# Dealing the late layout of a mixture's blocks out between the chunks of its first blocks

## The chip, the cores and the metric

One core of one Trainium2 chip. The metric is the device time of one launch in microseconds (us), the median of the runs shown. In the profile the engines are PE (TensorE, matmuls), PEld (its weight loads), DVE (VectorE), ACT (ScalarE), POOL (GpSimd) and SP (SyncE, which here mostly issues DMAs).

## The reference

x is 4 x 1024 x 128, float32. A layer normalisation feeds a mixture of experts, an attention follows, and then the same mixture again:

```python
x = x + 0.5 * ffn(layernorm(x))
x = x + attn(layernorm(x))
x = x + 0.5 * ffn(layernorm(x))
```

`ffn` normalises its rows once more, computes eight router logits a token, keeps the two largest, and adds the two experts' outputs weighted by a softmax of the two. An expert (D = 128, H = 512) normalises, then computes

```python
x1 = x @ W1 + b1
x2 = clip(x @ W2 + b2, -20, 20)
hidden = clip(x1 * (x2 * sigmoid(x2)), -10000, 10000)
return clip(hidden @ Wo + bo, -10000, 10000)
```

`attn` is an attention of 16 heads of 8 in which queries, keys and values are the same projection.

## The kernel before, in words

**Routing.** The first mixture routes its 4096 tokens in four batches of 1024 (`first_routing`, four jobs of 13 steps). For each token and choice DVE works out the place of its row, and POOL scatters 128 rows at a time to DRAM (L1296, 16 scatters a batch), where each expert has a region of its own. All engines run the same list of steps in the same order, each doing its own part.

**Blocks.** The rows are then worked off in 40 blocks: blocks 0 to 22 and 31 to 39 of 256 rows, blocks 23 to 30 of 128. Which expert and which rows a block takes depends on the routing. DVE works it out on one partition and leaves it in `whose_i`, where SP reads it into a register for the two loads of a block, the expert's weights (`ffn_rec`, L958, four slots in this mixture) and the rows (`ffn_block_rows`, L963, six slots).

**The two layouts.** `vector_lay_out_early` lays out blocks 0 to 16 (`EARLY` = 17) from the counts of the first three batches. `vector_lay_out_late` lays out blocks 17 to 39 from the counts of all four. It has nine pieces (`share(part, 9)`), 47 small DVE instructions, most of them on one partition and 8 to 46 elements, a few on up to 368. Most wait for the one before it: `settle` adds a semaphore signal to an instruction and makes DVE wait for it. Piece 0 begins with `end_i` (L1790), which signals `laid_out`; SP waits for that before the fillers of blocks 8 to 15. Piece 8 ends with `whose_i` (L1871), which signals `laid_out` again; SP waits for that before the loads of block 17. Its buffers are small tiles of their own and one partition of two routing buffers that nothing else uses in that time.

In the program before, DVE runs the whole late layout in one go, behind the last routing step and ahead of `vector_experts(0)`.

**A block.** `tensor_experts`, `scalar_experts` and `vector_experts` go through the 40 blocks, with four chunks of the hidden units in each (c = 0 to 3). The order on each engine is fixed:

- PE, block i: chunk 0 (two products, L2188 and L2190), turn back block i-2 (L2210), turn block i+1 (L2141), chunks 1 and 2, second product of block i-1 (L2200, eight matmul records), chunk 3. A chunk has one of four PSUM banks and waits until the combination of four chunks before has emptied it.
- DVE, block i: clip of chunk 0 (L1917), combination of block i-1's chunk 3 (L1928), clip of block i-1's hidden units (L1936), clip of chunk 1, combination 0, clip 2, combinations 1 and 2, clip of block i-1's y (L1943), clip 3.
- ACT: the silu of each chunk (L1455), the copy of the turned rows (L1409), the bias (L1464) and the weighting (L1473) of y.
- POOL: scatters the finished rows of y (L1312), two blocks behind.

The second product of block i-1 waits for the clipped hidden units, these for the combination of chunk 3, that for the silu of chunk 3, and that for the clip of chunk 3.

**Chores.** Between the chunks each engine calls `tail(k, i, c)`: a list of chores for mixture k, block i, ahead of chunk c. For the first mixture the lists are `HEAD`, for blocks 1 to 39, with index 4 * (block - 1) + c. Before the change they hold the last batch's 14 remaining scatters, the wait for the first turned blocks, the blanking of attention's buffers from block 16 on, and, from block 31, the beginning of attention. A chore is a tuple (what, which, step, part); each engine does what it has for it, and the chore "lay" is known to DVE alone (`vector_chore`), with which = 0 for the early and 1 for the late layout. In the second mixture the lists are `TAIL`, with index 4 * block + c, and the late layout is already dealt out there, one piece in each of the slots 40, 42, ... 56, that is, ahead of chunks 0 and 2 of blocks 10 to 14.

Of the kernel before, what the change touches and what calls it, by code (L numbers as in the profile page):

```python
# [88 lines left out]
def build_macaron(nc, x, w_qkv, w_o, ln_g, ln_b, router_w, eg, eb, w1, b1, w2, b2, wo, bo, out):  # L89
# [83 lines left out]
    with stack:  # L173
# [509 lines left out]
        HEAD = [[] for _ in range(HC * (BLOCKS - BEGIN))]  # L683

        def plan_head(block, slots):
            for slot, what, which, step in slots:
                HEAD[HC * (block - BEGIN) + slot].append((what, which, step, WHOLE))
# [3 lines left out]
        FIRST_OUT = 2  # L691
        for block in range(BEGIN, BEGIN + 3):
            plan_head(block, [(0, "turned", block, 0)])
        for n in range(FIRST_OUT, BT * TOPK):
            HEAD[HC * (n - FIRST_OUT)].append(("route", JOBS[B - 1], ROUTE_STEPS - 1, (n, BT * TOPK)))
        plan_head(16, [(HC * n, "blank", n, 0) for n in range(6)])
# [70 lines left out]
        def first_routing():  # L767

            def steps(b, which):
                if b < B:
                    for k in which:
                        yield "route", JOBS[b], k, WHOLE

            def scatters(b, part):
                yield "route", JOBS[b], SCATTER, (part, 6)

            def folds(pieces):
                for n in pieces:  # L780
                    if n <= E:
                        yield "fold", n, 0, WHOLE

            yield from steps(0, range(6))
            yield from steps(1, (0,))
            yield from steps(0, (6,))
            yield from steps(1, (1,))
            yield from steps(0, range(7, SCATTER))
            yield from folds((0,))
            for b in range(1, B):  # L790
                yield from steps(b, (2,))
                yield from folds((3 * b - 2,))
                yield from scatters(b - 1, 0)
                yield from steps(b, (3, 4))
                yield from scatters(b - 1, 1)
                yield from steps(b, (5,))
                yield from folds((3 * b - 1, 3 * b))
                yield from steps(b + 1, (0,))
                yield from steps(b, (6,))
                yield from scatters(b - 1, 2)  # L800
                yield from steps(b + 1, (1,))
                yield from steps(b, (7,))
                yield from scatters(b - 1, 3)
                yield from steps(b, (8, 9))
                if b == B - 1:
                    yield "folded", 0, 0, WHOLE
                yield from scatters(b - 1, 4)
                yield from steps(b, (10, 11))
                if b == B - 2:
                    yield "lay", 0, 0, WHOLE  # L810
                yield from scatters(b - 1, 5)
# [753 lines left out]
        def settle(instruction):  # L1565
            instruction.then_inc(dve_own.sem, 1)
            V.wait_ge(dve_own.sem, dve_own.up())

        def vector_program():
            V.wait_ge(pool_made, 3)  # L1570
            V.tensor_copy(region[:, :], regions[:, :])
            V.tensor_copy(block_f[:, :], blocks_i[:, 0, :])
            V.tensor_copy(tile_f[:, :], blocks_i[:, 1, :])
            settle(V.tensor_reduce(out=order[:, :], in_=not_later[:, :, :].rearrange("p i j -> p j i"), axis=AX.X, op=ALU.add))
            settle(V.memset(running[:, :, :], 1.0))
            V.memset(running[:, :, 0:1], 0.0)
            V.memset(twice[:, :], 1.0)
            V.memset(skipped[:, :, :], 0.0)
            V.memset(ends[:, :, 0:1], 0.0).then_inc(dve_made, 1)
            V.wait_ge(dve_made, 1)  # L1580
            for what, which, step, part in first_routing():
                if what == "route":
                    vector_route(which, step, part)
                elif what == "lay":
                    vector_lay_out_early()
                elif what == "folded":
                    vector_fold()
            vector_lay_out_late()
            vector_experts(0)
            vector_attention()  # L1590
            vector_experts(1)
            vector_last_sums()

        def vector_fold():
            V.wait_ge(fold_act, 1)
            V.wait_ge(fold_pe, 1 + E)
            bias = [record[:, :, at:at + HC] for at in (BIAS1, BIAS2)]
            for k in range(2):
                V.tensor_tensor(bias[k], wide[1][:, k * 512:k * 512 + E * HC].rearrange("p (e c) -> p e c", c=HC),
                                b_col[k].rearrange("p (e c) -> p e c", c=HC), ALU.add).then_inc(fold_dve, 1)  # L1600
            V.wait_ge(fold_dve, 2)
            V.tensor_copy(record[:, :, BO], bo_col)
            V.tensor_scalar(record[:, :, CLIP_LO:CLIP_LO + HC], bias[1], -1.0, -X2_LIMIT,
                            ALU.mult, ALU.add).then_inc(fold_dve, 1)
            V.tensor_scalar(record[:, :, CLIP_HI:CLIP_HI + HC], bias[1], -1.0, X2_LIMIT,
                            ALU.mult, ALU.add).then_inc(fold_dve, 1)
# [150 lines left out]
        def vector_lay_out_early(part=WHOLE):  # L1757


            for at in share(part, 8):  # L1760
                if at == 0:
                    settle(V.tensor_tensor(tiles_f[:, :], carry[0:1, :], region[0:1, :], ALU.subtract))
                    V.tensor_copy(tiles_i[:, :], tiles_f[:, :])
                    settle(V.tensor_scalar(firsts_f[:, :], first_rows[:, :], float(BLOCK - 1), None, ALU.add))
                    settle(V.tensor_copy(firsts_i[:, :], firsts_f[:, :]))
                elif at == 1:
                    V.tensor_scalar(firsts_i[:, :], firsts_i[:, :], BLOCK.bit_length() - 1, None,
                                    ALU.logical_shift_right)
                    settle(V.tensor_scalar(pairs_i[:, :], tiles_i[:, :], BLOCK.bit_length() - 1, None,
                                           ALU.logical_shift_right))  # L1770
                    V.tensor_copy(pairs_f[:, :], pairs_i[:, :])
                    settle(V.tensor_copy(firsts_f[:, :], firsts_i[:, :]))
                elif at == 2:
                    vector_pairs(0, EARLY)
                elif at == 3:
                    V.tensor_tensor(taken[:, :], got[:, 0:E], got[:, E:2 * E], ALU.add)
                    settle(V.tensor_tensor(skipped[:, 0, E:2 * E], ends[:, 0, E:2 * E], got[:, 0:E], ALU.subtract))
                    settle(V.tensor_copy(skipped[:, 0, 0:E], ends[:, 0, 0:E]))
                    settle(V.tensor_scalar(skipped[:, 0, :], skipped[:, 0, :], float(BH), None, ALU.mult))
                elif at < 7:  # L1780
                    vector_places_of_blocks(at - 3, 0, 1)
                else:
                    vector_whole_places(0, 1)
# [94 lines left out]
        def vector_experts(k):  # L1878
            if k == 0:

                V.wait_ge(fold_act, 1 + E)
                V.wait_ge(fold_dve, 4)
                for job in JOBS[1:B - 1]:
                    for lane in set_of(job).rows_out:
                        V.wait_ge(lane, 16 * BT)
            for i in range(BLOCKS):
                vector_tail(k, i, 0)
                vector_clip(k, i, 0)
                if i:
                    vector_combine(k, i - 1, 3)  # L1890
                    vector_clip_hidden(k, i - 1)
                vector_tail(k, i, 1)
                vector_clip(k, i, 1)
                vector_combine(k, i, 0)
                vector_tail(k, i, 2)
                vector_clip(k, i, 2)
                vector_combine(k, i, 1)
                vector_combine(k, i, 2)
                if i:
                    vector_clip_y(k, i - 1)  # L1900
                vector_tail(k, i, 3)
                vector_clip(k, i, 3)
            vector_combine(k, BLOCKS - 1, 3)
            vector_clip_hidden(k, BLOCKS - 1)
            vector_clip_y(k, BLOCKS - 1)
# [488 lines left out]
```

## Time and profile before

| | |
|---|---|
| median of 3 runs | 1370.96 us (1369.79, 1370.96, 1371.23) |
| the profiled execution | 1381.39 us |
| its span (first to last instruction) | 1379.3 us |
| mean granted TensorE clock | 0.978 |
| PE busy | 1245.2 us (90%) |
| DVE busy | 1156.8 us (84%) |
| ACT busy | 893.9 us (65%) |
| POOL busy | 534.9 us (39%) |
| chain that ended last, by engine | PE 57%, DVE 21%, issue 10%, ACT 4%, DMA 3%, SP's queue 3% |

The profiled execution is one run of its own and 10 us longer than the median of the others. Its times are counted from the first instruction. In it the first mixture's blocks begin at about 105 us, attention at about 340 us, and the second mixture's late layout is worked off between 1195 and 1224 us. A row of the trace has the start of an instruction or a group of them, its duration, its engine and its line, what it writes and reads, and, in brackets, how long the engine sat idle ahead of it and what ended that. Instructions of one engine overlap a little in these rows.

### The profile page before, as it was taken

The page shows a single profiled execution, that of the slowest core. Times are in us where ns is not written, and L with a number is a line of the kernel's source. Part 1 is how long each engine was busy: PE and PEld are TensorE (multiplying, and loading weights), DVE is VectorE, ACT ScalarE, POOL GpSimd, SP SyncE. Part 2 cuts the span into 40 slices and gives each one's busy share as a digit, 9 for nine tenths or more (in the row PEclk, how much of TensorE's full clock was granted, in tenths as well). Part 3 has the DMA queues.
Part 4 walks back from the last instruction along what each step waited for, and adds up shares of the span by engine and source line. Part 5 has one row for each costly group of instructions (what it writes and reads, how often), then busy time and mean ns, then how long its engine had stood idle before and what let it go on. Part 6 is the DMA issues. An engine that isn't in the chain of part 4 may idle for free.

```text
span 1379.3 us, 29625 instructions
## 1 busy us (share of the span) xinstructions
PE 1245.2 (90%) x10053; PEld 645.8 (47%) x10053; DVE 1156.8 (84%) x2354; ACT 893.9 (65%) x1881; POOL 534.9 (39%) x665
## 2 busy tenths in 40 slices
PE   3738999888699999999999999999999989999993
PEld 3737888776123223322323323233322247778882
DVE  8768888787998998889898888988899647988885
ACT  1214555554288888888788787788877874555651
POOL 3872557253542002234234424333443215553332
PEclk9999999999599999999999999999999999999996
DMA  8125655553212200112011011011100222555653
GB/s 272 42 70 186 208 206 189 214 190 104 72 37 60 67 28 12 36 38 73 19 45 49 13 59 37 21 33 54 36 3 20 104 82 105 189 186 200 232 209 131
DMA packets 65383, 135.58 MB, mean 98 GB/s; under 512 B 13330, under 2 KB 34932, under 8 KB 65204
## 3 DMA queue, kind: packets, MB, share of 16 engines
q1 hardware_dynamic: 56052, 115.39, 24.5%
q0 software_dynamic: 8704, 16.93, 3.7%
q8 instruction: 83, 1.36, 0.4%
q10 hardware_dynamic: 480, 1.38, 0.3%
q14 instruction: 64, 0.52, 0.1%
HBM read 47.35 MB, written 25.07 MB: 53 GB/s over the span
## 4 chain that ended last, share of the span: by engine, by line
PE 57%; DVE 21%; issue 10%; ACT 4%; DMA 3%; SPq 3%; POOL 1%; DVEq 0%; ACTq 0%; another core or an unknown queue 0%; POOLq 0%
PE psum L2290 14%; DVE att_neg_part L1976 11%; PE psum L2266 8%; PE psum L2200 7%; PE psum L2188 6%; PE psum L2190 6%; PE psum L2270 5%; PE psum L2247 5%; DMA ffn_block_rows<-rows_dram 2%; DVE att_neg_part L1981 2%; DVE ffn_x2c L1917 2%; DVE ffn_hidden L1928 1%; DVE stats L1610 1%; ACT att_probs L1488 1%; PE psum L2313 1%
## 5 line engine op out<-in xcount | busy, mean ns | idle before, releaser
L1488 ACT ACTIVATE att_probs<-psum 128x512 f32<-128x512 f32 x1024 | 556.3, 596 | 118.5 <-PE psum L2272 88.4
L1976 DVE TENSOR_REDUCE att_neg_part<-psum 128x2 f32<-128x1024 f32 x443 | 534.9, 1223 | 59.3 <-PE psum L2248 45.9
L2290 PE MATMUL psum<-att_probs,att_values 128*16 128x256 f32 x4096 | 320.3, 385 | 6.2 <-ACT att_o_t L1503 4.0
L1455 ACT ACTIVATE ffn_silu<-ffn_x2c,ffn_rec 128x256 f32<-128x256 f32 (+1 forms) x320 | 154.9, 487 | 173.0 <-DVE ffn_x2c L1917 128.1
L1312 POOL DMA_INDIRECT y_dram<-ffn_y,ffn_block_rows x144 | 143.7, 998 | 239.8 <-ACT ffn_y L1473 203.6
L2247 PE MATMUL psum<-att_right,att_left 64*128 64x512 bf16 x512 | 197.9, 388 | 13.6 <-DVE att_neg_part L1976 8.5
L2269 PE MATMUL psum<-att_right,att_left 64*128 64x512 bf16 x512 | 198.9, 388 | 4.2 <-DVE att_neg_part L1976 2.5
L2266 PE MATMUL psum<-att_right,att_left 64*128 64x512 bf16 x512 | 198.9, 388 | 4.1 <-DVE att_neg_part L1976 3.7
L2248 PE MATMUL psum<-att_right,att_left 64*128 64x512 bf16 x512 | 198.4, 388 | 0.0
L2270 PE MATMUL psum<-att_right,att_left 64*128 64x512 bf16 x512 | 193.9, 379 | 0.0
L2272 PE MATMUL psum<-att_right,att_left 64*128 64x512 bf16 x512 | 193.7, 378 | 0.0
L1917 DVE TENSOR_SCALAR ffn_x2c<-psum,ffn_rec 128x256 f32<-128x256 f32 (+1 forms) x320 | 162.8, 513 | 36.7 <-PE psum L2190 29.4
L2188 PE MATMUL psum<-ffn_block_t,ffn_rec 128*128 128x256 f32 (+1 forms) x640 | 179.6, 363 | 1.3 <-ACT ffn_block_t L1409 1.3
L1296 POOL DMA_INDIRECT rows_dram<-rows,place_i x128 | 126.6, 989 | 135.6 <-PE psum L2272 85.7
L2190 PE MATMUL psum<-ffn_block_t,ffn_rec 128*128 128x256 f32 (+1 forms) x640 | 178.9, 361 | 0.0
L2290 PEld LDWEIGHTS psum<-att_probs,att_values 128*16 128x16 f32 x4096 | 68.1, 94 | 221.9 <-issue 151.6
L1928 DVE SCALAR_TENSOR_TENSOR ffn_hidden<-psum,ffn_rec,ffn_silu 128x256 f32<-128x256 f32 (+1 forms) x320 | 144.3, 451 | 19.0 <-ACT ffn_silu L1455 11.9
L2200 PE MATMUL psum<-ffn_hidden,ffn_rec 128*128 128x256 f32 (+1 forms) x640 | 142.7, 367 | 14.3 <-DVE ffn_hidden L1936 10.6
L2266 PEld LDWEIGHTS psum<-att_right,att_left 64*128 64x128 bf16 x512 | 47.4, 93 | 196.7 <-ACT att_probs L1488 124.6
L1214 POOL TENSOR_TENSOR att_max_rest<-att_max_rest,att_max_parts 16x128 f32<-16x128 f32 x64 | 26.7, 417 | 276.8 <-ACT att_max_parts L1562 274.0
L2200 PEld LDWEIGHTS psum<-ffn_hidden,ffn_rec 128*128 128x128 f32 x640 | 112.0, 193 | 36.0 <-DVE ffn_hidden L1936 18.6
L2190 PEld LDWEIGHTS psum<-ffn_block_t,ffn_rec 128*128 128x128 f32 x640 | 118.2, 193 | 13.5
(222 smaller groups left out, 1522.3 us busy)
## 6 DMA issues: line engine op xcount, KB each, us to landing
ffn_rec<-record SPq DMA_DIRECT2D x80, 776.5 KB
ffn_block_rows<-rows_dram SPq DMA_DIRECT2D x64, 130.0 KB
att_left<-q_parts_dram SPq DMA_DIRECT2D x64, 96.0 KB
att_right<-q_parts_dram SPq DMA_DIRECT2D x124, 48.0 KB
record<-in_L_ffn_W SPq DMA_DIRECT2D x16, 256.0 KB, 6.4
att_right<-q_parts_dram SPq DMA_DIRECT2D x92, 32.0 KB
y_dram<-ffn_y,ffn_block_rows POOLq DMA_INDIRECT x144
q_parts_dram<-att_parts SPq DMA_DIRECT2D x12, 192.0 KB
```

The costliest lines, as they stand in the source:

```text
L1488: S.activation(probs[:, slot % PROBS, :], ring_bank(("score", slot))[:, :], ACT.Exp, scale=SCALE).then_inc(att_bank.by_act, 1)
L1976: last = V.tensor_reduce(out=neg_part[:, h % 2, keys, p::PAIR, t], in_=psum[:, low:high + 1, :], axis=AX.X, op=ALU.max, negate=True)
L2188: TE.matmul(both[:, few], mix[k].rec[:, s, W2 + c * P:W2 + (c + 1) * P], mix[k].block_t[:, m % 2, few], start=True, stop=True)
L2190: TE.matmul(both[:, w1_few], mix[k].rec[:, s, W1 + c * P:W1 + (c + 1) * P], mix[k].block_t[:, m % 2, few], start=True, stop=True).then_inc ...
L2200: last = TE.matmul(y_bank[n % 2][:, few], mix[k].rec[:, s, WO + c * F:WO + (c + 1) * F], mix[k].hidden[:, n % 2, c, few], start=(c == 0), ...
L2247: TE.matmul(bank[low], left[s][TOP, p, q], right[s][TOP, p, k], start=True, stop=True)
L2248: TE.matmul(bank[high], left[s][BOTTOM, PAIR + p, q], right[s][BOTTOM, PAIR + p, k], start=True, stop=True).then_inc(maxed, 1)
L2266: TE.matmul(low, left[s][TOP, p, k], right[s][TOP, p, q], start=True, stop=False)
L2269: TE.matmul(high, left[s][BOTTOM, PAIR + p, k], right[s][BOTTOM, PAIR + p, q], start=True, stop=False)
L2270: TE.matmul(low, left[s][TOP, PAIR + p, k], right[s][TOP, PAIR + p, q], start=False, stop=True).then_inc(att_bank.filled, 1)
L2272: TE.matmul(high, left[s][BOTTOM, p, k], right[s][BOTTOM, p, q], start=False, stop=True).then_inc(att_bank.filled, 1)
L2290: last = TE.matmul(value_bank[head * VS:head * VS + VW, q], values[:, b % 2, kt, team * TEAM + head, :], probs[:, (UNIT * n + j) % PROBS, ...
```

## The change

The call of `vector_lay_out_late` ahead of the blocks goes. In its place nine chores ("lay", 1, 0, (k, 9)) are appended to the lists 1, 6, 11, 16, 21, 26, 31, 36 and 41 of `HEAD`.

```diff
         FIRST_OUT = 2
         for block in range(BEGIN, BEGIN + 3):
             plan_head(block, [(0, "turned", block, 0)])
+        for k in range(9):
+            HEAD[1 + 5 * k].append(("lay", 1, 0, (k, 9)))
         for n in range(FIRST_OUT, BT * TOPK):
             HEAD[HC * (n - FIRST_OUT)].append(("route", JOBS[B - 1], ROUTE_STEPS - 1, (n, BT * TOPK)))
...
                     vector_lay_out_early()
                 elif what == "folded":
                     vector_fold()
-            vector_lay_out_late()
             vector_experts(0)
             vector_attention()
             vector_experts(1)
```

## Rows read from the trace of the kernel before

**Rows 1.** Stretch, us; busy PE, PEld, DVE, ACT, POOL; granted clock, DMA share, GB/s.

```profile
135.00:152.00 17.00, 17.00 (x87) 14.98 (x86) 14.07 (x32) 9.94 (x25) 8.80 (x9) 1.00 0.58 204
```

**Rows 2.** Timeline of DVE, 95 to 114 us: start, duration, instruction.

```profile
96.16 0.37 DVE L1790 CAST end_i<-carry 1x8 int32<-1x8 f32 x1
...
105.73 0.15 DVE L1813 TENSOR_TENSOR skipped<-ends,taken 1x8 f32<-1x8 f32 x1
...
106.96 0.22 DVE L1849 TENSOR_TENSOR xf_t<-block_f,ends 1x96 f32<-1x96 f32 x1
...
108.22 0.52 DVE L1855 TENSOR_REDUCE whose<-xf_t 1x23 f32<-1x368 f32 x1
...
109.34 0.17 DVE L1859 TENSOR_SCALAR of_the_second_half<-whose 1x23 f32<-1x23 f32 x1
...
110.64 0.17 DVE L1867 TENSOR_SCALAR whose<-whose 1x23 f32<-1x23 f32 x1
...
111.52 1.04 DVE L1917 TENSOR_SCALAR ffn_x2c<-psum,ffn_rec 128x256 f32<-128x256 f32 x2
...
113.61 0.55 DVE L1917 TENSOR_SCALAR ffn_x2c<-psum,ffn_rec 128x256 f32<-128x256 f32 x1 [0.49 <-PE psum L2190]
```

**Rows 3.** Timeline of PE, 109 to 118 us.

```profile
109.58 0.69 PE L2141 MATMUL psum<-identity,ffn_block_rows 128*128 128x128 f32 x2 [0.91 <-DMA ffn_block_rows<-rows_dram]
...
117.51 1.99 PE L2200 MATMUL psum<-ffn_hidden,ffn_rec 128*128 128x256 f32 x8 [0.27 <-DVE ffn_hidden L1936]
```

**Rows 4.** The chain that ended last, in order of time: start, us, what.

```profile
115.13 0.55 DVE ffn_x2c L1917
...
116.24 0.50 DVE ffn_hidden L1928
116.76 0.70 DVE ffn_hidden L1936
...
129.02 1.73 PE psum L2200 x8
```

**Rows 5.** Timeline of DVE in a block without a chore, 126 to 132 us.

```profile
126.03 0.54 DVE L1917 TENSOR_SCALAR ffn_x2c<-psum,ffn_rec 128x256 f32<-128x256 f32 x1
126.89 0.54 DVE L1917 TENSOR_SCALAR ffn_x2c<-psum,ffn_rec 128x256 f32<-128x256 f32 x1 [0.32 <-PE psum L2190]
127.35 0.47 DVE L1928 SCALAR_TENSOR_TENSOR ffn_hidden<-psum,ffn_rec,ffn_silu 128x256 f32<-128x256 f32 x1
127.86 0.69 DVE L1936 TENSOR_SCALAR ffn_hidden<-ffn_hidden 128x1024 f32<-128x1024 f32 x1
...
131.29 0.29 DVE L1943 TENSOR_SCALAR ffn_y_t<-ffn_y_t 128x256 f32<-128x256 f32 x1 [0.38 <-ACT ffn_y_t L1464]
131.65 0.54 DVE L1917 TENSOR_SCALAR ffn_x2c<-psum,ffn_rec 128x256 f32<-128x256 f32 x1
```

**Rows 6.** Timeline of DVE in the second mixture, pieces 0, 1 and 2.

```profile
1195.81 0.15 DVE L1790 CAST end_i<-carry 1x8 int32<-1x8 f32 x1
...
1196.88 0.54 DVE L1917 TENSOR_SCALAR ffn_x2c<-psum,ffn_rec 128x256 f32<-128x256 f32 x1
...
1199.31 0.14 DVE L1798 SCALAR_TENSOR_TENSOR tiles_f<-taken,tiles_f 1x8 f32<-1x8 f32 x1
...
1200.82 0.54 DVE L1917 TENSOR_SCALAR ffn_x2c<-psum,ffn_rec 128x256 f32<-128x256 f32 x1
...
1203.00 0.14 DVE L1835 TENSOR_TENSOR pairs_in_order<-firsts_f,pairs_f 1x8 f32<-1x8 f32 x1
...
1203.97 0.54 DVE L1917 TENSOR_SCALAR ffn_x2c<-psum,ffn_rec 128x256 f32<-128x256 f32 x1
```

**Rows 7.** Timeline of PE in the second mixture, two second products.

```profile
1198.60 1.99 PE L2200 MATMUL psum<-ffn_hidden,ffn_rec 128*128 128x256 f32 x8 [1.26 <-DVE ffn_hidden L1936]
...
1205.69 1.99 PE L2200 MATMUL psum<-ffn_hidden,ffn_rec 128*128 128x256 f32 x8 [0.63 <-DVE ffn_hidden L1936]
```

**Rows 8.** POOL's row scatters, 88 to 103 us: ns min/median/max, first and last start.

```profile
L1296 POOL DMA_INDIRECT rows_dram<-rows,place_i x12: 954/958/961, 88.0 to 101.9; - x12
```

## The prediction

> **What bounds the kernel now.** I read the stretch around the change first, then the place the change writes to, then a later stage of the same program that already does what the change asks for. In blocks 3 to 6 of the first mixture PE is busy 17.00 of 17 us and DVE 14.07 [rows 1]: PE is the bound, a block takes it 5.62 us (from one clip of chunk 3 to the next, 131.65 - 126.03 [rows 5]), and DVE has under a fifth of each block to spare. Ahead of the blocks DVE is alone with the late layout, from 96.16 on; its first clip starts at 111.52, right behind it [rows 2]. So the layout looks as if it held the mixture up. It doesn't: PE has nothing to multiply until block 0's rows land, it then waits 0.91 us for block 1's rows, by DMA [rows 3], and DVE, once in the loop, waits 0.49 us for PE at the clip of chunk 2 (113.61 [rows 2]). From there the order of the work is the same with or without the layout.
>
> **What the change removes.** 15.36 us of DVE in one piece (96.16 to 111.52 [rows 2]). What it uncovers: chunk 0's product ended at 108.67 (109.58 - 0.91 [rows 3]), so the first clip may start 2.85 us earlier. The next ones, and the first silu and combination, move up too, but the clip of chunk 2 needs a product that came later than DVE did, by 0.49 us. Everything behind (the silu, the chunk 3 clip at 115.13, the combination at 116.24 [rows 4], the clipped hidden block, PE's second product at 117.51 [rows 3]) hangs on that clip. I cost the gain at 0. Its bounds are 0 and 2.85 us. The SP queue's loads of the first four blocks wait for the early layout and for scatters, not for this one; the fillers and block 17 do wait for it, and it ends in block 11, so five blocks (28 us) ahead of the last of those needs. The layout's two signals to SP move with it; no DMA and no PE, ACT or POOL instruction does.
>
> **What it adds.** The same instructions, in nine pieces, in front of a clip each. Block and chunk by the index 1 + 5k: piece 0 in block 1 chunk 1, then 2/2, 3/3, 5/0, 6/1, 7/2, 8/3, 10/0, 11/1. Their lengths, from first instruction to the next clip: the second mixture deals out the same nine pieces, and there pieces 0, 1, 2 take 1.07 (1196.88 - 1195.81), 1.51 (1200.82 - 1199.31) and 0.97 us (1203.97 - 1203.00) [rows 6]. The others from the layout itself [rows 2]: pieces 3 and 4 together 1.23 (106.96 - 105.73), piece 5 1.26, piece 6 1.12, piece 7 1.30, piece 8 0.88. For pieces 0 to 2 the layout's own rows give 9.57 us (105.73 - 96.16) instead of 3.55: that stretch has pauses between tiny instructions that the second mixture has not. I take the dealt-out lengths, because the work around them is the same; the other value is the upper end.
>
> **What covers a piece.** In a block without one [rows 5]: 0.32 us of waiting for PE before the clip of chunk 0, 0.38 us before the clip of y, 0.07 us between that and the clip of chunk 3. A row that reads PSUM reaches 0.08 into the next when they are packed (126.89 + 0.54 against 127.35), so these are room for 0.40, 0.46 and 0.15. Between the clip of chunk 3 and its combination lie 1.32 us (127.35 - 126.03), where the fastest is 1.11 (116.24 - 115.13 [rows 4]): a late clip of chunk 3 recovers only 0.21 on that way. Last, the hidden block is clipped at 128.55 (127.86 + 0.69 [rows 5]) and PE wants it at 129.02 [rows 4]; 0.05 goes to the signal (116.76 + 0.70 [rows 4] is followed by 117.51 [rows 3]), so 0.41 or 0.42 is slack; I take 0.41. The room is therefore
> - ahead of chunk 1 or 2: 0.46 + 0.15 + 0.21 + 0.41 = 1.23;
> - ahead of chunk 3: 0.15 + 0.21 + 0.41 = 0.77;
> - ahead of chunk 0: 0.40 + 0.41 = 0.81.
>
> What is over stops PE; after a stop DVE is still 0.41 late, which the next block takes back if nothing comes first. Queued behind a piece on DVE are exactly this clip, the silu of ACT and, last, PE's second product.
>
> **A test of this rule.** In the second mixture piece 1 stands ahead of a chunk 2 and piece 2 ahead of the following chunk 0, DVE coming in 0.41 late. The rule says 0.41 + 1.51 - 0.46 - 0.15 = 1.31, then - 0.40 + 0.97 = 1.88, then - 0.41 = 1.47 us of stop. PE's second products start at 1198.60 and 1205.69 [rows 7]: 7.09 - 5.62 = 1.47.
>
> **The sum.** Piece 0: DVE comes in late by 0.15 (its slack of 0.41 is used up by the stop of 0.27 before 117.51, and PE's slow restart, 1.99 against 1.73 for the eight products [rows 3, 4], gives 0.26 back). 0.15 + 1.07 = 1.22, under 1.23: no cost, 0.40 stays open. Piece 1: 0.40 + 1.51 - 1.23 = 0.68. Piece 2: the open 0.41 is taken back ahead of the clip of y, 0.97 - 0.77 = 0.20. Pieces 3 and 4: at most 0.7 each, covered by 0.81 and 1.23. Piece 5: 1.26 - 1.23 = 0.03. Piece 6: 1.12 - 0.77 = 0.35. Piece 7: 1.30 - 0.81 = 0.49. Piece 8: 0.88, covered. Together 1.75. A restart of PE costs 0 to 0.26 (1.99 - 1.73); the row of a packed group overlaps its neighbours, so I take 0.10, and count it for pieces 2, 6 and 7, where no further piece follows at once: 0.30. **Sum +2.05 us**, against the profiled execution's 1381.39 us (span 1379.3). The median of the runs is 1370.96, 10.4 us lower; the stage is PE-bound in both, so I carry the term over unchanged: 1370.96 + 2.05 = 1373.0. Nothing later has room to take it back: every later stage starts from the blocks before it. A measurement of this kernel can tell about 0.2%, 2.7 us, from no change, so the forecast lies just inside "no change".
>
> **A rule weighed.** Of POOL's twelve row scatters between 88 and 103 us the first seven run ahead of the layout and the others beside it, and all take the same: 954 to 961 ns [rows 8]. The layout doesn't hold them up, so nothing is released when it goes. The Trainium skill (SBUF — State Buffer, "Who interferes with whom") says that a DVE copy, cast or tensor_scalar in a mode that uses two ports locks GpSimd out for the whole instruction, which would delay its writing of descriptors. By that rule the start would gain; the trace does not bear it out here.
>
> **Rivals.**
> 1. *Slower: the pauses come along.* Pieces 0 to 2 keep the length they have in the layout, 9.57 us for 3.55, and the 6.02 us more go straight to PE, since the room is used up: +2.05 + 6.02 = 8.1, 1379.0. For it: the pauses sit in exactly these instructions. Against: the same instructions have none in the second mixture, nor pieces 3 to 8 in the layout. It decides as soon as a piece in blocks 1 to 3 is 0.7 us longer than taken. Chance 0.14.
> 2. *Faster: the early first clip counts.* If PE's pace or its second product follows DVE after all, the 2.85 us come through: 1370.2 with the pieces' cost, 1368.1 if those are hidden too. Against: the 0.49 us wait at 113.61 and PE's wait for DMA at 109.58. Chance 0.08.
> 3. *All pieces hidden.* DVE's share of 14.07 in 17 leaves 0.97 us a block, 10.7 us in eleven blocks, more than the 9.3 us of pieces. By the average they fit: 1371.0. Against: the test above, where spare time that lies behind the hidden block doesn't help it. Chance 0.09.
> 4. *The scatters were held.* The five scatters beside the layout, freed of up to 0.37 us each (its first instruction [rows 2]), would bring the rows 1.9 us earlier: 1373.0 - 1.9 = 1371.1. Against: rows 8. The Trainium skill's rule above is this case. Chance 0.03.
>
> **How the numbers follow.** The forecast has 0.66. Its own spread is the restart (0 to 0.26 five times) and some 0.1 a piece, from +1.3 to +3.5, so about a quarter of it lies above +2.7. Slower by over 0.2%: 0.14 + 0.66 x 0.24 = 0.30. Faster by over 0.2% (under 1368.2): half of rival 2, 0.04. Within: 0.66. The range goes from 1369.8 (rivals 3 and 4, less the 1.2 us by which a run of before lies under the median) to 1376.5 (the forecast's upper end and half of what rival 1 adds).
>
> **What would show it.** DVE's first clip near 108.7 us and PE's first second product still at 117.5; no PE wait in blocks 1, 4, 6 and 11; waits of PE for the hidden block of 0.5 to 0.8 us by piece 1 (block 2's second product), and of 0.2 to 0.6 us behind pieces 2, 6 and 7; attention starting 2 us later. It is wrong if PE's second product of block 0 moves, if PE has no stop by piece 1, or if a piece in blocks 1 to 3 lasts over 2 us.

## The result, and the profile after

The changed kernel takes **1374.20 us**, the median of eight runs (1372.89 to 1377.16), and the kernel before 1370.27 us, the median of eight beside them (1368.70 to 1373.86). The ratio is 1.003, with a 95% interval from 1.0018 to 1.0042, so the change costs 3.9 us, between 2.5 and 5.8. That is slower by more than 0.2%, the case that had 0.30. The time lies inside the range, 1.2 us above the forecast; the forecast's sum of 2.05 us is about half of what was lost. That the time itself came so close is in part luck: beside it the kernel before took 0.7 us less than the 1370.96 us that the forecast started from.

The profiled execution of the changed kernel took 1375.75 us, span 1373.7. This is **less** than the 1381.39 us (span 1379.3) of the profiled execution of before, while the medians stand the other way round. So the two profiles can't be subtracted as wholes; they have to be compared stage by stage. The top of the page of the changed kernel:

```profile
span 1373.7 us, 29625 instructions
PE 1245.5 (91%) x10053; PEld 644.2 (47%) x10053; DVE 1154.9 (84%) x2354; ACT 893.3 (65%) x1881; POOL 533.2 (39%) x665
```

The instruction counts are those of before and the busy times differ by 2 us at most. The change shows only in where the engines stand idle. The windows view of the eleven blocks and a little behind them (stretch; busy PE, PEld, DVE, ACT, POOL; granted clock, DMA share, GB/s) has PE idle for 2.36 us of 77 where the same stretch of the kernel before, in a second profile of it taken later (run e10_before), has 0.26. After:

```profile
113.00:190.00 77.00, 74.64 (x365) 63.34 (x364) 68.78 (x175) 42.06 (x105) 35.40 (x36) 1.00 0.56 191
```

Before, second profile:

```profile
113.00:190.00 77.00, 76.74 (x381) 67.45 (x381) 63.65 (x138) 44.42 (x108) 37.25 (x38) 1.00 0.57 196
```

The view of waits names what stopped PE in that stretch of the changed kernel (us in total, times, longest):

```profile
PE psum L2201 <- DVE ffn_hidden L1937: 1.6, 3, 0.6
PE psum L2211 <- DVE ffn_y_t L1944: 0.8, 1, 0.8
```

Three of the four are waits of the second product for the clipped hidden block, as the prediction had them. The fourth, the longest, isn't: PE's turn back waits for the clipped y. Both are on PE's timeline (start, duration, instruction, idle before it and its releaser). Each second product is the eight matmuls of one block:

```profile
112.40 1.99 PE L2201 MATMUL psum<-ffn_hidden,ffn_rec 128*128 128x256 f32 x8 [0.26 <-DVE ffn_hidden L1937]
118.13 1.91 PE L2201 MATMUL psum<-ffn_hidden,ffn_rec 128*128 128x256 f32 x8
...
122.53 0.44 PE L2211 MATMUL psum<-identity,ffn_y_t 128*128 128x128 f32 x2 [0.77 <-DVE ffn_y_t L1944]
124.77 1.99 PE L2201 MATMUL psum<-ffn_hidden,ffn_rec 128*128 128x256 f32 x8
...
131.16 2.00 PE L2201 MATMUL psum<-ffn_hidden,ffn_rec 128*128 128x256 f32 x8 [0.51 <-DVE ffn_hidden L1937]
...
160.68 1.99 PE L2201 MATMUL psum<-ffn_hidden,ffn_rec 128*128 128x256 f32 x8 [0.49 <-DVE ffn_hidden L1937]
...
167.16 1.99 PE L2201 MATMUL psum<-ffn_hidden,ffn_rec 128*128 128x256 f32 x8 [0.60 <-DVE ffn_hidden L1937]
```

These groups make a clock for the stage. An undisturbed block lasts 5.62 us from the end of one group to the end of the next ([rows 5] give the same period from DVE). Block 2's ends at 126.76 and block 1's at 120.04: 6.72 us, an **excess** of 1.10. Summed over blocks 1 to 11 the excess is 4.2 us. In both profiles of the kernel before it is zero there. A second profile of the changed kernel, taken later (e11_after), gives 4.25 us, block for block within 0.08. Nothing takes it back up to block 24: from block 0's group to block 24's it is 130.79 and 130.77 us in the two profiles of before, 134.99 and 135.03 in the two of the changed kernel. From block 25 on, two profiles of one and the same kernel differ by 0.7 to 3.9 us in this measure, so they can't follow it further. The runs lost 3.9 us, which agrees with it.

The start of the blocks is the other place to look. In the profile of before, PE's first turn began at 105.40 and the first second product at 117.51 [rows 3], 12.11 us later. Here PE reads

```profile
102.65 0.66 PE L2142 MATMUL psum<-identity,ffn_block_rows 128*128 128x128 f32 x2 [12.26 <-DMA ffn_block_rows<-rows_dram]
```

and the second product is at 112.40, 9.75 us later; PE turns block 1 at 105.78 without the 0.91 us wait for its rows. One of the prediction's signs of being wrong has come up: "if PE's second product of block 0 moves". Read alone, this says that the change won 2.4 us at the start and lost 6.3 us in the blocks.

### The profile page after: what moved, and what is told of

Same layout as the page of the kernel before. It is cut to its first block, busy times and chain, and to the rows that moved or that the text cites. A ratio compares the mean times of both kernels' runs of the same rounds, so it can differ in the third digit from the quotient of the medians.

```text
span 1373.7 us, 29625 instructions
## 1 busy us (share of the span) xinstructions
PE 1245.5 (91%) x10053; PEld 644.2 (47%) x10053; DVE 1154.9 (84%) x2354; ACT 893.3 (65%) x1881; POOL 533.2 (39%) x665
## 4 chain that ended last, share of the span: by engine, by line
PE 56%; DVE 25%; issue 5%; POOL 5%; ACT 4%; DMA 4%; SPq 1%; DVEq 0%; ACTq 0%; POOLq 0%
PE psum L2291 14%; DVE att_neg_part L1977 11%; PE psum L2267 8%; PE psum L2201 7%; PE psum L2189 5%; PE psum L2191 5%; PE psum L2271 5%; PE psum L2248 5%; POOL rows_dram L1298 3%; DVE ffn_x2c L1918 2%; DMA ffn_block_rows<-rows_dram 2%; DVE att_neg_part L1982 2%; DVE ffn_hidden L1929 2%; DVE stats L1611 1%; ACT ffn_silu L1457 1%
```

## The experiments

Two readings had to be told apart, and one more came up on the way.

- **Theory A**, the prediction's: the layout ahead of the blocks costs nothing, and the whole loss is PE stopped by the dealt-out pieces. The quicker start in the profile is chance.
- **Theory B**: the layout in front does hold up the start, by 2.4 us (12.11 against 9.75), and the pieces cost 6.3. B2 is its small form, a gain of about 0.7 us.
- **Theory L**, formed on the changed kernel's trace: a scatter on POOL holds up DVE's clip of y, which reads and writes SBUF alone, if the clip comes at a bad moment, and pieces bring it there.

The level of the kernel before was different from one group of runs to the next (1370.3, 1379.6, 1388.5 and 1370.9 us). The last three groups ran on three different chips. Every time is therefore set against the runs of before of its own group. A kernel without any late layout (e1_none) was to measure the front part by itself; it gave no time and decides nothing.

### The pieces alone: e2_twice

The layout is called ahead of the blocks, as before, and the nine pieces are dealt out as well, as a repetition without signals.

```
+    vector_lay_out_late()                              # ahead of vector_experts(0)
-    HEAD[1 + 5 * k].append(("lay", 1, 0, (k, 9)))
+    HEAD[1 + 5 * k].append(("lay", 2, 0, (k, 9)))      # 2: vector_lay_out_late(part, signal=False)
```

> The late layout stands ahead of the blocks as before and is dealt out a second time in the changed kernel's places, the second time without its signals. This adds the pieces alone. Theory A: the same time as the changed kernel, +4.2 us to before, 1374.5, with the PE stops of the changed kernel (0.77 for the turn back, 0.5, 0.5 and 0.6 for the hidden block). Theory B: 2.4 us slower than the changed kernel, 1376.6.

Measured: 1382.46 us against 1379.58; ratio 1.0034, interval 1.0021 to 1.0047. Its excess is 4.22 us in the pattern of the changed kernel, and its start is that of before (12.24 us). The waits of PE in the blocks:

```profile
PE psum L2209 <- DVE ffn_hidden L1945: 1.8, 4, 0.6
PE psum L2219 <- DVE ffn_y_t L1952: 0.8, 1, 0.8
```

With the front part in place and the pieces added, the loss is the whole loss of the change. The ratio 1.0034 beside 1.003 leaves little room for a gain of 2.4 us from taking the front away.

### The pieces elsewhere, and finer: e3_chunk1, e4_fine

e3_chunk1 deals the same nine pieces ahead of chunk 1 of blocks 1 to 9, where the prediction's table has the largest room, 1.23 us:

```
-    HEAD[1 + 5 * k].append(("lay", 1, 0, (k, 9)))
+    HEAD[1 + 4 * k].append(("lay", 1, 0, (k, 9)))
```

> The same nine pieces, each ahead of chunk 1 of blocks 1 to 9. The prediction's rooms (1.23 us ahead of chunk 1) with the lengths of the changed kernel's trace (1.07, 1.69, 0.97, 0.61, 0.54, 1.38, 1.10, 1.28, 0.67) give 0.4 of lateness open from piece 0, then 0.86 for piece 1, 0.15 for piece 5, little for 7: about +1.2 us to before, with restarts of 0.26 each +1.8. If the pieces cost by their length and not by their place, it is +4.2 us as in the changed kernel.

Measured: 1380.60 us against 1379.58, ratio 1.0015 (1.0007 to 1.0024), excess 1.91 us. The waits:

```profile
PE psum L2211 <- DVE ffn_y_t L1944: 0.3, 1, 0.3
PE psum L2201 <- DVE ffn_hidden L1937: 0.3, 1, 0.3
```

Same work, same number of pieces, half the loss, by place alone. Piece 2 tells something more. It follows a stop, comes in 0.15 us late and lasts 0.98, together 1.13 us, under the room of 1.23, and still it costs 0.17.

e4_fine also goes to chunk 1, but in thirteen pieces: pieces 1, 5, 6 and 7 are each cut in two, so that none lasts longer than about 1.0 us.

```
+    for k in range(13):
+        HEAD[1 + 4 * k].append(("lay", 2, 0, (k, 13)))     # pieces 1, 5, 6 and 7 cut in two
```

> The layout in 13 pieces (pieces 1, 5, 6 and 7 cut in two), each ahead of chunk 1 of blocks 1 to 13, none longer than about 1.07 us. All are under the room of 1.23 us; with 0.28 us more for a DVE instruction that POOL holds up, only piece 0 may touch it. Theory A: the time of before, 1370.3 to 1371, and no PE stop over 0.2 us. Theory B: 2.4 us faster than before, 1367.9. If a piece costs whatever its length, +3 us or more.

Measured: 1377.14 us against 1379.58, ratio 0.9992 (0.9981 to 1.0004), excess 0.05 us in all, and one wait of PE in the stretch, the one ahead of block 0's second product that every kernel here has:

```profile
PE psum L2252 <- DVE ffn_hidden L1988: 0.2, 1, 0.2
```

The layout dealt out finely enough costs nothing, and brings nothing that this run can tell. Eleven more runs beside seventeen of the kernel before (e9_fine_again) narrow that down.

> The 13 short pieces once more, against the kernel before. Its nine stops are gone (0.05 to 0.2 us in the first look), so this measures what taking the layout from ahead of the blocks gives by itself. In the looks so far the way from the first turned rows to the first second product takes 12.1 to 12.2 us with the whole layout ahead and 9.8 to 11.7 without, and PE waits 0.8 to 1.0 us for block 1's rows with it and 0 to 0.4 without. Theory A (no gain; the differences are those of single executions): 0 to before, interval around it. Theory B2 (a small gain of some 0.7 us, which the changed kernel also has): -0.7 us. A gain of 2.4 us: -2.4 us.

Measured: 1370.64 us against 1370.89, ratio 0.9997 (0.9988 to 1.0006), excess 0.11 us. Under Theory B this kernel, with the front part gone and pieces that cost nothing, should have shown a gain of 2.4 us (0.9982); that lies outside the interval. B2's 0.7 us (0.9995) can't be excluded.

### The front doubled: e5_front_twice

The layout stands ahead of the blocks twice, and nothing is dealt out.

```
+    vector_lay_out_late()
+    vector_lay_out_again(WHOLE)        # the same, without signals; then vector_experts(0)
```

> The late layout runs twice in a row ahead of the blocks, the second time without its signals, nothing dealt out. It tells how much cover the place ahead of the blocks has. The second run's 47 instructions take 9.3 us where they aren't paused (the sum of the nine dealt-out lengths). If the cover is the 0.5 us by which DVE was early at the clip of chunk 2, DVE is late there by about 9 us and so is the first second product: about 21 us after the first turned rows, against 12.1 to 12.2 with one layout ahead; total +9 us. If DVE's work ahead of the blocks is hidden more deeply (behind PE's half pace or the loads), less than +5 us.

Measured in one run: 1392.59 us against a median of 1388.47 (1384.75 to 1392.52). The first second product comes 20.9 us after the first turn, 8.8 later than the 12.1 of before. PE's timeline:

```profile
108.04 0.66 PE L2149 MATMUL psum<-identity,ffn_block_rows 128*128 128x128 f32 x2 [12.39 <-DMA ffn_block_rows<-rows_dram]
...
124.52 1.19 PE L2196 MATMUL psum<-ffn_block_t,ffn_rec 128*128 128x256 f32 x2 [6.77 <-DVE ffn_hidden L1936]
...
128.51 0.59 PE L2198 MATMUL psum<-ffn_block_t,ffn_rec 128*128 128x256 f32 x2
128.94 1.89 PE L2208 MATMUL psum<-ffn_hidden,ffn_rec 128*128 128x256 f32 x8
```

So DVE in front does hold PE up once it is long enough: PE fills the banks that it has and stops at the next chunk. One layout ends before that point, two don't. After the stop of 6.77 us PE runs at half pace, two products in 1.19 us and then in 0.59. The windows of the two stretches show it in the granted clock, 0.50 (1.2 GHz) and 1.00 (2.4 GHz):

```profile
124.50:127.50 3.00, 2.98 (x8) 2.44 (x9) 2.55 (x6) 1.36 (x4) 0.00 (x0) 0.50 0.00 0
128.00:131.00 3.00, 3.00 (x16) 2.64 (x15) 2.55 (x6) 1.15 (x3) 0.00 (x0) 1.00 0.00 0
```

The one time is only 4.1 us above the median of its group, whose runs spread over 7.8 us; it decides nothing.

### Three pieces put back: e6_front3

Pieces 0 to 2 return to the front, the others stay dealt out.

```
+    for k in range(3): vector_lay_out_late((k, 9))     # ahead of vector_experts(0)
+    for k in range(3, 9): HEAD[1 + 5 * k].append(("lay", 1, 0, (k, 9)))
```

> Pieces 0 to 2 ahead of the blocks, pieces 3 to 8 dealt out where the change has them. By the stops in the changed kernel's trace pieces 3 to 8 make 2.1 of the 4.2 us (0.34 behind piece 5, 0.89 behind 6, 0.86 behind 7), so: +2.1 us to before, and no stop in blocks 1 to 5. By the prediction's terms: +0.9 and 0.2 of restarts, +1.1 us.

Measured: 1389.26 us against 1388.47, ratio 1.001 (0.9994 to 1.0026), excess 2.23 us: the stops of pieces 1 and 2 are gone, and those of 5, 6 and 7 stand unchanged (0.34, 0.90, 0.86). Another 0.12 is seen at block 4's second product, which stands behind chunk 0 of block 5, where piece 3 is (0.67 us long here). The pieces don't act on one another across the blocks without a piece between them.

### What stretches the clip of y: e7_act_out

The DVE timeline of the changed kernel has something that the one of before [rows 5] lacks. This is piece 1 and what follows it:

```profile
118.75 0.14 DVE L1799 SCALAR_TENSOR_TENSOR tiles_f<-taken,tiles_f 1x8 f32<-1x8 f32 x1
...
119.39 0.42 DVE L1805 CAST firsts_i<-firsts_f 1x8 int32<-1x8 f32 x1
...
120.44 0.54 DVE L1918 TENSOR_SCALAR ffn_x2c<-psum,ffn_rec 128x256 f32<-128x256 f32 x1
...
121.96 0.52 DVE L1944 TENSOR_SCALAR ffn_y_t<-ffn_y_t 128x256 f32<-128x256 f32 x1
...
127.31 0.57 DVE L1944 TENSOR_SCALAR ffn_y_t<-ffn_y_t 128x256 f32<-128x256 f32 x1 [0.24 <-ACT ffn_y_t L1466]
...
139.50 0.29 DVE L1944 TENSOR_SCALAR ffn_y_t<-ffn_y_t 128x256 f32<-128x256 f32 x1 [0.23 <-ACT ffn_y_t L1466]
```

The clip of y takes 0.29 us in an undisturbed block [rows 5] and 0.52 and 0.57 here; a cast of eight elements takes 0.42 where its neighbours take 0.15. POOL's timeline has the scatters that were under way:

```profile
121.42 0.97 POOL L1298 DMA_INDIRECT rows_dram<-rows,place_i  x1 [0.30 <-issue]
...
126.77 0.99 POOL L1314 DMA_INDIRECT y_dram<-ffn_y,ffn_block_rows  x1 [0.30 <-issue]
...
139.18 0.99 POOL L1314 DMA_INDIRECT y_dram<-ffn_y,ffn_block_rows  x1 [0.30 <-issue]
```

The two long clips start 0.54 us into a scatter, the short one 0.32. Over the profiles, clips that start up to 0.47 us into one take 0.29; at 0.54 to 0.56 they take 0.52 to 0.57, at 0.65 0.45, at 0.70 0.40, at 0.80 0.31, and later 0.28. The exception is one clip near block 14 in ten of the profiles, those of before too, which starts at 0.46 to 0.48 and takes 0.62 to 0.64; why this one isn't known. Starts at 0.46, 0.54 and 0.70 that are held all end 1.1 us after the scatter's start: the clip doesn't run slowly, it is held until then. In the kernel before the clips of y up to there start at 0.44 to 0.48 (but one, at 0.99), just ahead of the bad stretch. In the changed kernel seven of them fall into it.

This test takes the y scatters away from POOL: ACT's queue writes the y rows out in order by plain DMAs, so that the rows of the output are not put at their places.

```
+    S.dma_start(y_dram[k][at:at + P, :], mix[k].y[:, n % YSETS, r, :])     # ACT, in scalar_weigh
-    pool_scatter_results(k, at - 2)
+    G.wait_ge(weighed, k * BLOCKS + at - 1)
```

> The changed kernel with the finished rows of y written out by ACT's DMA queue to fixed rows instead of scattered by POOL, in both mixtures (so attention reads them in another order and the output is another). POOL's row scatters of the last batch stay. Theory L (a DVE instruction between two SBUF tiles that meets the later part of a POOL scatter waits for it, which lengthens the clip of y from 0.29 to 0.52 to 0.57 us): the clips of y in blocks 2 to 12 take 0.29 us, and the stops behind pieces 1, 2, 5 and 6 shrink by up to 0.28 each: the excess of the nine pieces goes from 4.2 to 3.2 us or a little under. If the long clips come from something else (a late y from ACT, DMA traffic), they stay, and the excess stays at 4.2.

Measured: all clips of y take 0.28 to 0.30 us, and the excess falls from 4.2 to 2.86 us. Piece 1 and its clip of y once more, now the cast with 0.15 us and the clip with 0.29, and then the waits of PE that are left:

```profile
127.62 0.15 DVE L1803 SCALAR_TENSOR_TENSOR tiles_f<-taken,tiles_f 1x8 f32<-1x8 f32 x1
...
128.26 0.15 DVE L1809 CAST firsts_i<-firsts_f 1x8 int32<-1x8 f32 x1
...
128.99 0.54 DVE L1922 TENSOR_SCALAR ffn_x2c<-psum,ffn_rec 128x256 f32<-128x256 f32 x1
...
130.51 0.29 DVE L1948 TENSOR_SCALAR ffn_y_t<-ffn_y_t 128x256 f32<-128x256 f32 x1
```

```profile
PE psum L2205 <- DVE ffn_hidden L1941: 1.1, 3, 0.5
PE psum L2215 <- DVE ffn_y_t L1948: 0.2, 1, 0.2
```

Piece 1 lasts 1.37 us (127.62 to 128.99) instead of 1.69 (118.75 to 120.44), and its excess falls by 0.55: 0.32 of the piece and 0.23 of the clip (0.52 less 0.29). So the hold is worth 1.32 us of the 4.18 in all. The one time, 1384.25 us against 1388.47, isn't used, since this kernel's output work is another.

### The rooms measured by themselves: e8_rooms

On the kernel before, rows of tiny instructions with no other purpose are put ahead of single chunks: eight at a time (1.51 us on the undisturbed row below) ahead of block 2 chunk 0, block 4 chunk 1, block 6 chunk 2 and block 8 chunk 3, and five at a time (0.93 and 1.19 us in two of their places) ahead of block 9 chunk 0, 11/1, 13/2 and 15/3.

```
+    for c in range(4):
+        plan_head(2 + 2 * c, [(c, "room", 8, 0)])
+        plan_head(9 + 2 * c, [(c, "room", 5, 0)])
+    # "room": settle(V.tensor_scalar(second[:, 0:E], second[:, 0:E], 1.0, None, ALU.mult)), `which` times
```

> The kernel before, with the layout ahead of the blocks, and eight dummy pieces of tiny DVE instructions (one waiting for the other, 0.19 us each): eight of them ahead of block 2 chunk 0, 4/1, 6/2, 8/3 (about 1.52 us), and five ahead of 9/0, 11/1, 13/2, 15/3 (about 0.96 us). The stop is the length less the room of the place, plus a restart. By the prediction's rooms and a restart of 0.26: 1.52 us gives 0.97, 0.55, 0.55, 1.01; 0.96 us gives 0.41, 0, 0, 0.45. If the turn back of y is what stops PE at chunks 1 and 2 the room is 1.30 there, nearly the same sum, but the stop is seen at the turn back. A clip of y held up by POOL adds 0.28 at chunks 1 to 3.

Measured by excess: 1.00 us for block 2 chunk 0, where the rooms and a restart of 0.26 give 1.51 - 0.81 + 0.26 = 0.96; 0.59 for block 4 chunk 1 (1.51 - 1.23 + 0.26 = 0.54); none for 11/1. Block 13 chunk 2 (1.19 us) has 0.28 where the rule with a room of 1.23 gives none. 8/3 and 9/0 turned out to follow each other directly, so their 2.04 us together test neither. The other two were stretched by POOL. On DVE's timeline, the undisturbed eight, the eight of block 6 and the five of block 15:

```profile
140.05 1.51 DVE L2000 TENSOR_SCALAR of_the_second_half<-of_the_second_half 1x8 f32<-1x8 f32 x8
...
152.73 1.77 DVE L2000 TENSOR_SCALAR of_the_second_half<-of_the_second_half 1x8 f32<-1x8 f32 x8
...
208.93 1.73 DVE L2000 TENSOR_SCALAR of_the_second_half<-of_the_second_half 1x8 f32<-1x8 f32 x5
```

and what POOL did beside the last:

```profile
209.19 2.93 POOL L1167 MEMSET att_values<- 128x256 f32 x8
```

The clip of y isn't the only instruction that is held. Two scatters of y, from 152.95 and 154.24, lie over block 6's eight, which cost 1.08 us (the clip of y behind them was held too, 0.52 us); block 15's five have a scatter from 208.23 and then the memsets beside them and cost 1.31. How much of the 1.73 is due to which of the two isn't told apart.

### Both kernels once more: e10_before, e11_after

> The kernel before, unchanged, for a second profile of it. Theory A: PE's wait for block 1's rows and the 12.1 us from the first turned rows to the first second product differ from execution to execution and may come out as 11.3 to 11.7 too. Theory B2: they come out at 0.8 to 1.0 and 12.0 to 12.3 us again, as in all executions with the layout ahead.

> The changed kernel once more. The excess of blocks 2 to 12 again 4.2 us, as the order of the work on each engine sets it. The start: 9.8 us from the first turned rows to the first second product if that is a property of the change, 11.3 to 11.7 if it was this one execution's. Time: +3.5 to +4.2 us to before.

Measured: 1374.92 us for the changed kernel against 1370.89, ratio 1.0032 (1.0020 to 1.0044), excess 4.25. One run of the kernel before: 1369.32 us, excess 0.01. Its start is what matters here (PE):

```profile
102.99 0.66 PE L2141 MATMUL psum<-identity,ffn_block_rows 128*128 128x128 f32 x2 [12.43 <-DMA ffn_block_rows<-rows_dram]
...
113.40 1.99 PE L2200 MATMUL psum<-ffn_hidden,ffn_rec 128*128 128x256 f32 x8 [0.26 <-DVE ffn_hidden L1936]
```

That is 10.41 us with the layout in front, without the wait for block 1's rows. On DVE the layout has run without a pause, from its first to its last instruction in 8.9 us, where it took 15.3 in the profile of before (15.4 to the first clip, [rows 2]: 96.16 to 111.52), and the first clip waits for PE:

```profile
93.25 0.15 DVE L1790 CAST end_i<-carry 1x8 int32<-1x8 f32 x1
...
101.95 0.17 DVE L1871 CAST whose_i<-whose 1x46 int32<-1x46 f32 x1
...
106.40 0.55 DVE L1917 TENSOR_SCALAR ffn_x2c<-psum,ffn_rec 128x256 f32<-128x256 f32 x1 [4.27 <-PE psum L2190]
```

So neither the 12.11 us nor the pauses in the layout belong to every execution of this kernel. The pauses weren't a single case either: the layout in front took 14.4, 14.6 and 14.0 us in e2_twice, e5_front_twice (its first) and e8_rooms, while no dealt-out piece has them in any profile. The start took 12.24 us in e2_twice, 12.08 in e8_rooms and 10.41 here with the layout in front; 9.75 and 9.82 in the changed kernel, 11.35 in e3_chunk1, and 11.74 and 10.82 in the two profiles of the fine version, with it dealt out. In every profile with over 11.4 us PE waited for block 1's rows. The start varies by 1.7 us for the kernel before (12.11 and 10.41) and by 0.9 for the fine version. Within the last group, on one chip, the layout in front (10.41) stands between the nine pieces (9.82) and the thirteen (10.82). A difference of some 0.6 us between the quickest starts may be real; the runs of e9_fine_again are too coarse to tell it.

## Why the prediction was half right

**The place and the sign of the loss: right, and shown.** PE is the bound, the front layout costs nothing measurable (e2_twice, e9_fine_again; 0.7 us are not excluded), and the loss is PE stopped behind too little room, above all by pieces 1, 2, 6 and 7, with 0, 4 and 8 covered. Dealing to chunk 1 halves the loss, and cutting the long pieces removes it. Rival 3 (all hidden) and rival 2 (the early first clip counts) fall.

**The rooms: right in kind, each 0.16 us too large.** e8_rooms gives 1.00 and 0.59 us of excess where the rooms 0.81 and 1.23 give 0.96 and 0.54 with a restart of 0.26. But the slack of 0.41 in every room rests on 129.02 as the time at which PE wants the hidden block [rows 4], and in the chain of waits an instruction's row begins only where the row before it ends. The timelines of the kernel before have the clip of the hidden block (DVE) and the second product (PE) of an undisturbed block as

```profile
122.24 0.69 DVE L1936 TENSOR_SCALAR ffn_hidden<-ffn_hidden 128x1024 f32<-128x1024 f32 x1
123.23 1.89 PE L2200 MATMUL psum<-ffn_hidden,ffn_rec 128*128 128x256 f32 x8
```

The clip ends 0.30 us ahead of the product (122.93 and 123.23), and a product that waits starts 0.05 behind it: the slack is 0.25. For the same reason the eight matmuls are to be compared by 1.99 and 1.89, both from the timeline, and not by 1.99 and 1.73: a restart costs 0.10. For a piece that is over both rooms the two accounts give the same, 0.26 - 0.41 = 0.10 - 0.25. For a piece between them they don't, and there three runs bear out the smaller rooms, 1.07, 0.61 and 0.65 ahead of chunks 1 or 2, 3 and 0: piece 2 in e3_chunk1 (0.15 + 0.98 - 1.07 + 0.10 = 0.16, measured 0.17), block 13 in e8_rooms (1.19 - 1.07 + 0.10 = 0.22, measured 0.28) and piece 3 in e6_front3 (0.67 - 0.65 + 0.10 = 0.12, measured 0.12). The prediction took the large slack together with the small restart, and so lost 0.16 at each stop.

**The sum: too small, by these terms.** Predicted and measured excess by piece, us, and the terms of the rule with the smaller rooms and the lengths of e7_act_out:

| piece | predicted | measured | e7_act_out | rule, smaller rooms |
|---|---|---|---|---|
| 0 | 0 | 0.03 | 0.03 | 0 |
| 1 | 0.68 | 1.10 | 0.55 | 0.57 |
| 2 | 0.20 + 0.10 | 0.78 | 0.50 | 0.47 |
| 3 | 0 | 0.18 | 0.07 | 0 |
| 4 | 0 | 0 | 0 | 0 |
| 5 | 0.03 | 0.34 | 0.34 | 0.30 |
| 6 | 0.35 + 0.10 | 0.89 | 0.63 | 0.61 |
| 7 | 0.49 + 0.10 | 0.86 | 0.74 | 0.74 |
| 8 | 0 | 0 | 0 | 0 |
| sum | 2.05 | 4.18 | 2.86 | 2.69 |

1. *The step that failed* is "Queued behind a piece on DVE are exactly this clip, the silu of ACT and, last, PE's second product", together with durations taken as fixed. DVE's clip of y was costed at its 0.29 us of [rows 5]. A piece shifts it to 0.54 us into a scatter of POOL, and there it takes up to 0.57; the cast in piece 1 is held in the same way. With the y scatters gone the excess fell by 0.55 at piece 1, 0.28 at piece 2, 0.11 at piece 3, 0.26 at piece 6 and 0.12 at piece 7, 1.32 together. Behind piece 1 the late thing was then the clip of y itself, and PE stopped at its turn back, which the prediction had not counted among those that wait. The chain of waits of the changed kernel runs through it (start, us, what):

```profile
121.56 0.40 DVE ffn_hidden L1929
121.96 0.53 DVE ffn_y_t L1944
...
122.53 0.44 PE psum L2211 x2
```

2. *The restart and the slack.* The restart was put at 0.10 beside a slack of 0.41, as said above; that is 0.16 too little at pieces 2, 6 and 7, 0.48 us. At pieces 1 and 5 no restart was counted at all, 0.26 too little each, 0.52 us.

3. *Piece lengths.* Two lengths taken from the second mixture were too long, because pieces there had met scatters as well. Piece 0 was taken at 1.07. In the trace of before its long instruction (DVE) stands 0.53 us into a scatter (POOL):

```profile
1195.73 0.96 POOL L1296 DMA_INDIRECT rows_dram<-rows,place_i  x1 [1.11 <-DVE rows L1752]
1196.26 0.39 DVE L1794 TENSOR_SCALAR tiles_i<-tiles_i 1x8 int32<-1x8 int32 x1
```

In the changed kernel that instruction takes 0.16, and the piece 0.84, from its first row to the clip behind it:

```profile
112.26 0.15 DVE L1791 CAST end_i<-carry 1x8 int32<-1x8 f32 x1
...
113.10 0.54 DVE L1918 TENSOR_SCALAR ffn_x2c<-psum,ffn_rec 128x256 f32<-128x256 f32 x1
```

So piece 0 left 0.17 open for piece 1 and not 0.40 (measured 0.16: the second product of block 1 starts at 118.13, 0.14 us behind its clipped hidden block, in place of 0.30). Piece 1 was taken at 1.51 and lasts 1.37 free of the hold. Its term is 0.17 + 1.37 - 1.07 + 0.10 = 0.57, against 0.55 measured. The lengths take 0.36 us out of the sum.

That is 1.32 + 0.48 + 0.52 - 0.36 = 1.96 of the missing 2.13 us. The sign "no PE wait in blocks 1, 4, 6 and 11" held but for 0.18 in all at block 4's second product, which comes behind piece 3: DVE was late there from piece 2's stop and a held clip of y, and a room of 0.65 left too little for the piece's 0.62.

**Rival 1**, that the pauses come along, had the wrong ground: the kernel before doesn't have the pauses in e10_before, so they are no property of the layout's instructions. They came in four of the five profiles with the whole layout in front once or twice, and in no dealt-out piece; why stays open. **Rival 4** (scatters held by the layout) is not borne out at the start: the scatters beside the layout take no longer than those ahead of it [rows 8].

**The rule weighed** was read in one direction only. The Trainium skill (SBUF — State Buffer, "Who interferes with whom") says of the ports that DVE and GpSimd share that whoever comes first has them and the other blocks fully. The prediction tested whether POOL's scatters get longer, saw that they don't [rows 8], and dropped the rule. The other half of the same sentence bears on this case: the runs show DVE blocked, in a tensor_scalar and a cast from SBUF to SBUF, for up to 0.28 us. What they show beside the rule is that the scatter holds DVE in a part of its 0.98 us only, from about 0.5 to 1.1 us after its start. And the direction that the prediction tested is there after all in the blocks, only small: the six scatters, in four profiles, that start 0.05 to 0.09 us behind the start of a clip of y take 1.02 to 1.07 us. In the changed kernel (DVE, POOL):

```profile
151.59 0.28 DVE L1944 TENSOR_SCALAR ffn_y_t<-ffn_y_t 128x256 f32<-128x256 f32 x1
151.66 1.05 POOL L1298 DMA_INDIRECT rows_dram<-rows,place_i  x1 [0.30 <-issue]
```

**The sign "if PE's second product of block 0 moves"** was badly chosen. It moved, and the theory behind it still stood; one profile of each kernel can't carry a difference of 2.4 us in a stretch whose start varies by 1.7 for one kernel.

## What to carry to other kernels

When work is dealt out on an engine with a little spare time, what counts is not the spare share (here 0.97 us a block) but the room ahead of the one instruction whose lateness reaches the bound engine, and a piece that is longer than the room costs all that is over and a restart. Where pieces exceed the room, cut them: thirteen pieces of at most 1.0 us, ahead of chunk 1 with its 1.07, cost nothing that the runs can tell where nine cost 3.9 us. Read slack and restart from one and the same view, since the chain of waits cuts off the overlap that the timeline shows. An instruction that is shifted can change its duration as well, when another engine works on the same memory beside it, so look for its durations beside that engine's instructions before costing it by one row; here the trace of before had such a row already.

## What was not expected of the hardware

- The hold of DVE by POOL: a 128x256 f32 tensor_scalar within SBUF took 0.29 us, or up to 0.57 when it started 0.54 to 0.56 us into an indirect scatter. A cast of eight elements took 0.42 instead of 0.15. Five tiny tensor_scalars took 1.73 us beside a scatter and POOL's memsets, 0.92, 0.93 and 1.19 elsewhere.
- Stops of up to 0.8 us, several in the stretch, left the granted clock of TensorE at 1.00 (windows above), and cost a restart of some 0.10 us each (eight matmuls in 1.99 us against 1.89 in one timeline). A stop of 6.77 us was followed by 3 us at 0.50.
- A chain of tiny DVE instructions, each settled before the next, took 8.9 us in one execution of a kernel and 15.3 in another of the same, with pauses of 0.5 to 1.2 us between instructions, and 14.0 to 14.6 in three more profiles. This was not explained.
